# A ViT layer on one core: mean subtraction and rounding multiply of two activation quantisations moved from VectorE to GpSimd

## The reference

```python
def _act_quant(x):
    scale = 127.0 / jnp.clip(jnp.max(jnp.abs(x), axis=-1, keepdims=True), 1e-05)
    y = jnp.clip(jnp.round(x * scale), -128.0, 127.0) / scale
    return x + jax.lax.stop_gradient(y - x)

def _bitlinear(x, w):
    mu = jnp.mean(x, axis=(1, 2), keepdims=True)
    var = jnp.var(x, axis=(1, 2), keepdims=True)
    x_norm = (x - mu) * jax.lax.rsqrt(var + EPS)
    return _act_quant(x_norm) @ _weight_quant(w).T
...
q = _bitlinear(x, w_q).reshape(bsz, seq_len, NH, HD).transpose(0, 2, 1, 3)
...
return _bitlinear(out, w_o)
```

## Time and profile before

| | us |
|---|---|
| median of 3 runs | 2735.33 (2728.14 to 2740.37) |
| the profiled execution | 2730.84 |
| its span, first to last instruction | 2729.0 |
| DVE busy | 1579.2 |
| PE busy | 2267.6 |
| POOL busy | 818.9 |

### The profile page before, as it was taken

How to read it: one execution, slowest core, us unless ns; L and a number is a source line. 1 busy time by engine, 2 the same in 40 slices (tenths; PEclk the granted TensorE clock), 3 DMA queues, 4 the chain that set the end, 5 groups by cost and what they waited for, 6 DMA issues and landing times. The chain is left out here.

```text
span 2729.0 us, 46461 instructions
## 1 busy us (share of the span) xinstructions
PE 2267.6 (83%) x12048; PEld 1081.0 (40%) x12049; DVE 1579.2 (58%) x4148; ACT 1220.6 (45%) x2360; POOL 818.9 (30%) x718
## 2 busy tenths in 40 slices
PE   3798888887888888788888878878607999999998
PEld 2333333333333333333333333322204666666665
DVE  4567766676675667667666776776344333333332
ACT  1255545544454545445454544544323444444443
POOL 2112223031312313132221313212223555555554
PEclk9799889898988889789888989888758999999999
DMA  2222222222212222121222222121033333333332
GB/s 88 74 67 68 62 71 62 68 63 62 62 55 72 50 80 63 49 75 55 72 54 76 63 59 55 54 75 43 29 139 86 55 55 54 54 53 57 53 52 40
DMA packets 181078, 172.06 MB, mean 63 GB/s; under 512 B 40002, under 2 KB 169620, under 8 KB 180884
## 3 DMA queue, kind: packets, MB, share of 16 engines
q1 hardware_dynamic: 150612, 134.94, 17.2%
q0 software_dynamic: 30272, 34.80, 8.2%
HBM read 100.82 MB, written 68.93 MB: 62 GB/s over the span
## 5 line engine op out<-in xcount | busy, mean ns | idle before, releaser
L1106 DVE TENSOR_REDUCE mxs<-bank 128x1 f32<-128x512 f32 x1024 | 684.0, 686 | 476.1 <-PE bank L491 382.7
L804 ACT ACTIVATE pt<-bank 128x512 f32<-128x512 f32 x1024 | 588.2, 596 | 694.7 <-PE bank L500 634.2
L491 PE MATMUL bank<-ks,qs 96*128 96x512 bf16 x1024 | 430.4, 422 | 118.2 <-DVE mxs L1106 101.9
L500 PE MATMUL bank<-qs,ks 99*128 99x512 bf16 x1024 | 428.8, 420 | 6.6 <-ACT pt L804 5.4
L509 PE MATMUL bank<-pt,v_sb 128*32 128x512 f32 x2048 | 329.6, 721 | 0.0
L491 PEld LDWEIGHTS bank<-ks,qs 96*128 96x128 bf16 x1024 | 106.0, 104 | 496.0 <-DVE mxs L1106 344.1
L1642 POOL DMA_INDIRECT out<-y_sb,ids x136 | 215.3, 1583 | 273.2 <-DMA out<-y_sb,ids 210.7
L1688 PE MATMUL bank<-gu_h,xh 128*128 x544 | 208.2, 383 | 11.1 <-issue 7.9
L1767 DVE TENSOR_TENSOR hid_e<-bank,act_g 128x512 f32<-128x512 f32 x136 | 94.1, 692 | 210.7 <-PE bank L1688 210.7
L1771 DVE TENSOR_TENSOR hl<-bank,hh 128x512 bf16<-128x512 f32 x136 | 94.1, 692 | 210.0 <-ACT hh L1741 210.0
L966 POOL TENSOR_TENSOR cadd<-vcls,pr 128x256 f32<-128x256 f32 x64 | 40.6, 634 | 557.1 <-DVE pr L1138 556.8
(11 more groups left out here) (281 smaller groups left out, 3390.3 us busy)
## 6 DMA issues: line engine op xcount, KB each, us to landing
qs<-qk_dram SPq DMA_DIRECT2D x128, 128.0 KB, 2.4
ks<-qk_dram SPq DMA_DIRECT2D x64, 192.0 KB, 3.1
xt<-x_t SPq DMA_DIRECT2D x16, 512.0 KB, 4.1
h_dram<-h_sb SPq DMA_DIRECT2D x16, 512.0 KB, 3.4
qs<-qk_dram SPq DMA_DIRECT2D x128, 64.0 KB, 2.1
ks<-qk_dram SPq DMA_DIRECT2D x64, 128.0 KB, 3.0
hw<-h_dram SPq DMA_DIRECT2D x16, 512.0 KB, 5.6
out<-hw SPq DMA_DIRECT2D x16, 512.0 KB, 2.9
```

The lines of the kernel that those rows point to most:

```text
L491: mm(score[u % 2][:, :], qs[0:QK, h, blk(t)], ks[0:QK, h, :], start=True, stop=True) \
L500: mm(scoret[u % 2][:, :], ks[0:QK + MROWS, h, blk(t)], qs[0:QK + MROWS, h, :], start=True, stop=True).then_inc(s("pe_st"), 1)
L804: f(pt[:, t % 2, j, :], scoret[u % 2][:, :], ACT.Exp).then_inc(s("act_exp"), 1)
L1106: v.reduce_max(mxs[:, t, g * GH + j:g * GH + j + 1], score[u % 2][:, :], AX.X).then_inc(s("dve_mx"), 1)
```

## The change

The subtraction of the mean (lines 1273 and 1368) and the rounding multiplies (1285, 1394 and 1397) are taken from DVE's program and issued by POOL: at its places 13, 19, 46 and 52, each ahead of what POOL already did there. DVE signals `ms1`, `comb1` and `comb2` to POOL as it signalled others; its reductions at 15 and 49 wait for POOL's subtractions.

```diff
                     if P.ok and at == 13:
+                        hold(pool, s("dve_ms1"), 1, P, 1)
+                        hold(pool, s("act_xh"), TB, P, TB)
+                        g_.tensor_scalar(xn[:, :, :], xn[:, :, :], ms1[:, 0:1], None, ALU.subtract).then_inc(s("pool_xm"), 1)
                         rsqrt(rs1[:, :], msq1[:, 1:2], 1, 128, "dve_ve", "pool_rs", P)
                     if P.ok and at == 19:
-                        hold(pool, s("dve_q1"), TB, P, TB)
+                        hold(pool, s("dve_comb"), 1, P, 1)
+                        for t in range(TB):
+                            g_.tensor_scalar(xn[:, t, :], xn[:, t, :], comb1[:, t:t + 1], MAGIC, ALU.mult, ALU.add) \
+                                .then_inc(s("pool_q1"), 1)
+                        hold(pool, s("pool_q1"), TB, P, TB)
                         hold(pool, s("pe_xq"), 1, P, 0)
...
                     if W.ok and at == 46:
+                        hold(pool, s("dve_ms2"), 1, W, 1)
+                        g_.tensor_scalar(o_sb[:, W.par, :, :], o_sb[:, W.par, :, :], ms2[:, 0:1], None, ALU.subtract) \
+                            .then_inc(s("pool_om"), 1)
                         rsqrt(rs2[:, :], msq2[:, 1:2], 1, 128, "dve_ve2", "pool_rs2", W)
...
                     if W.ok and at == 52:
-                        hold(pool, s("dve_q2"), TB + 1, W, TB + 1)
+                        hold(pool, s("dve_comb2"), 1, W, 1)
+                        o = o_sb[:, W.par, :, :]
+                        for t in range(TB):
+                            g_.tensor_scalar(o[:, t, :], o[:, t, :], comb2[:, t:t + 1], MAGIC, ALU.mult, ALU.add) \
+                                .then_inc(s("pool_q2"), 1)
+                        cflat = oc[:, :, :].rearrange("p j d -> p (j d)")
+                        g_.tensor_scalar(cflat, cflat, comb2[0:NG, TB:TB + 1], MAGIC, ALU.mult, ALU.add) \
+                            .then_inc(s("pool_q2"), 1)
+                        hold(pool, s("pool_q2"), TB + 1, W, TB + 1)
                         hold(pool, s("pe_xqc"), 1, W, 0)
...
-                        wait(dve, s("act_xh"), TB, P, TB)
-                        v.tensor_scalar(xn[:, :, :], xn[:, :, :], ms1[:, 0:1], None, ALU.subtract).then_inc(s("dve_xm"), 1)
                     if P.ok and at == 15:
-                        wait(dve, s("dve_xm"), 1, P, 1)
+                        wait(dve, s("pool_xm"), 1, P, 1)
...
                     if P.ok and at == 18:
-                        for t in range(TB):
-                            v.tensor_scalar(xn[:, t, :], xn[:, t, :], comb1[:, t:t + 1], MAGIC, ALU.mult, ALU.add) \
-                                .then_inc(s("dve_q1"), 1)
...
-                    if W.ok and at == 48:
-                        o = o_sb[:, W.par, :, :]
-                        v.tensor_scalar(o, o, ms2[:, 0:1], None, ALU.subtract).then_inc(s("dve_om"), 1)
...
-                        wait(dve, s("dve_om"), 1, W, 1)
+                        wait(dve, s("pool_om"), 1, W, 1)
...
-                    if W.ok and at == 52:
-                        o = o_sb[:, W.par, :, :]
-                        for t in range(TB):
-                            v.tensor_scalar(o[:, t, :], o[:, t, :], comb2[:, t:t + 1], MAGIC, ALU.mult, ALU.add) \
-                                .then_inc(s("dve_q2"), 1)
-                        cflat = oc[:, :, :].rearrange("p j d -> p (j d)")
-                        v.tensor_scalar(cflat, cflat, comb2[0:NG, TB:TB + 1], MAGIC, ALU.mult, ALU.add) \
-                            .then_inc(s("dve_q2"), 1)
```

More of the change, by code:

```diff
@@ L1139, in normalise, with scales @@
             ch.end(2 * (g + 1))
-        def scales(ch, am, ax, rax, comb, aq, rs):
+        def scales(ch, am, ax, rax, comb, rs, done):
             ch(v.tensor_scalar(ax[:, :], am[:, :], rs[:, :], 1e-5, ALU.mult, ALU.max))
             ch(v.reciprocal(rax[:, :], ax[:, :]))
-            ch(v.tensor_scalar(comb[:, :], rax[:, :], 127.0, rs[:, :], ALU.mult, ALU.mult))
+            v.tensor_scalar(comb[:, :], rax[:, :], 127.0, rs[:, :], ALU.mult, ALU.mult).then_inc(s(done), 1)
         def token_stats(b, tiles_, np_, src, bn, chain, n):
@@ L1263, in body @@
                                                axis=AX.X, op=ALU.add), "dve_ms", 1, P, 1)
-                        ch = Link("dve_chain_p", 7, P)
-                        ch(v.scalar_tensor_tensor(ms1[:, :], red1[:, :], 1.0 / total, cls_f[:, 0:2], ALU.mult, ALU.add))
+                        ch = Link("dve_chain_p", 5, P)
+                        signal(v.scalar_tensor_tensor(ms1[:, :], red1[:, :], 1.0 / total, cls_f[:, 0:2], ALU.mult, ALU.add),
+                               "dve_ms1", 1, P, 1)
                         ch(v.tensor_tensor(msq1[:, 0:1], ms1[:, 0:1], ms1[:, 0:1], ALU.mult))
@@ L1271, in body @@
                                                   ALU.subtract, ALU.max))
-                        wait(dve, s("act_xh"), TB, P, TB)
-                        v.tensor_scalar(xn[:, :, :], xn[:, :, :], ms1[:, 0:1], None, ALU.subtract).then_inc(s("dve_xm"), 1)
+                        ch.end(3)
                     if P.ok and at == 15:
-                        wait(dve, s("dve_xm"), 1, P, 1)
+                        wait(dve, s("pool_xm"), 1, P, 1)
                         signal(v.tensor_reduce(out=am1[:, 0:TB], in_=xn[:, :, :], axis=AX.X, op=ALU.max,
@@ L1279, in body @@
                         wait(dve, s("pool_rs"), 1, P, 1)
-                        ch = Link("dve_chain_p", 7, P, 4)
-                        scales(ch, am1, ax1, rax1, comb1, aq1, rs1)
-                        ch.end(7)
+                        scales(Link("dve_chain_p", 5, P, 3), am1, ax1, rax1, comb1, rs1, "dve_comb")
                     if P.ok and at == 18:
-                        for t in range(TB):
-                            v.tensor_scalar(xn[:, t, :], xn[:, t, :], comb1[:, t:t + 1], MAGIC, ALU.mult, ALU.add) \
-                                .then_inc(s("dve_q1"), 1)
                         wait(dve, s("pe_aqb"), 1, P, 0)
@@ L1292, in body @@
                         ch = Link("dve_chain_c", 2, P)
+                        wait(dve, s("dve_comb"), 1, P, 1)
                         ch(v.tensor_scalar(cls_q[:, :], cls_t[:, :], ms1[:, 0:1], None, ALU.subtract))
@@ L1356, in body @@
                         signal(v.tensor_copy(ms2[:, :], d2[:, 0:2]), "dve_ms2", 1, W, 1)
-                        ch = Link("dve_chain_v", 6, W)
+                        ch = Link("dve_chain_v", 5, W)
                         ch(v.tensor_tensor(msq2[:, 0:1], ms2[:, 0:1], ms2[:, 0:1], ALU.mult))
@@ L1379, in body @@
                     if W.ok and at == 50:
-                        ch = Link("dve_chain_v", 6, W, 3)
+                        ch = Link("dve_chain_v", 5, W, 3)
                         wait(dve, s("pool_rs2"), 1, W, 1)
@@ L1386, in body @@
                                "dve_amx", 1, W, 1)
-                        scales(ch, am2, ax2, rax2, comb2, aqo, rs2)
-                        ch.end(6)
+                        scales(ch, am2, ax2, rax2, comb2, rs2, "dve_comb2")
+                        ch.end(5)
                         signal(v.tensor_scalar(aqo[:, :], ax2[:, :], 1.0 / 127.0, w_fac[:, 3:4], ALU.mult, ALU.mult),
                                "dve_aqo", 1, W, 1)
-                    if W.ok and at == 52:
-                        o = o_sb[:, W.par, :, :]
-                        for t in range(TB):
-                            v.tensor_scalar(o[:, t, :], o[:, t, :], comb2[:, t:t + 1], MAGIC, ALU.mult, ALU.add) \
-                                .then_inc(s("dve_q2"), 1)
-                        cflat = oc[:, :, :].rearrange("p j d -> p (j d)")
-                        v.tensor_scalar(cflat, cflat, comb2[0:NG, TB:TB + 1], MAGIC, ALU.mult, ALU.add) \
-                            .then_inc(s("dve_q2"), 1)
                     if P.ok and at == 50:
```

2 lines of the change are left out of this document (1 added, 1 removed).

## The result

| | before | after |
|---|---|---|
| median, both on the same chips | 2731.45 us (2727.13 to 2740.37) | 2745.18 us (2737.99 to 2758.16) |
| ratio, 95% interval | | 1.0051 (1.0029 to 1.0074) |
| profiled execution, its span | 2730.84, 2729.0 | 2741.06, 2739.2 |
| granted clock of TensorE in it | 0.892 | 0.885 |

The change makes the kernel about 14 us slower. The direction was wrong.

A forecast was written before the change was run, and what follows sets the result against it. PE, busy 83% of the span, was taken as the bound, with its waits for `qi` and `qic`. -1.2 us per image over fifteen images (-18) and +2 at the edges gave 2715 us profiled, 2719 us median; range 2692 to 2748.

The forecast's parts named there:

- How long the operations take on POOL: At the four places, a multiply on POOL takes 0.41 us (0.28 to 0.63), a subtraction 1.06 us.
- The shared resource: A DVE instruction touching only SBUF that starts inside a long POOL one ends some 0.03 us after it.
- Place 13: First subtraction: DVE's column steps end 0.9 us late, its subtraction slot of 0.67 us is saved; net +0.2 us per image.
- Places 17 to 20: First quantisation's multiplies, `comb1` to `qi`: 3.20 us becomes 3.24 us, +0.05 us per image.
- Places 46 to 49: Second subtraction: a DVE step is caught for +0.88 us, a slot of 0.66 us goes; net +0.2 us per image.
- Places 50 to 53: Second quantisation's multiplies, `comb2` to `qic`: 5.34 us becomes 3.69 us, -1.65 us per image.
- shows in the time one for one: At PE's waits for `qi` and `qic`, a change of the chain `ms` to `comb` to `qi` counts fully in the time.
- the clock recovers sooner: Rival, chance 0.15: less waiting shortens PE's half-clock stretch behind places 47 to 53, some 1.4 us per image more gained; 2698 us.
- Edges: First image at P and last at W, without attention beside them: POOL's slower operations are bare, some +2 us.
- Slow multiply: Rival, chance 0.17: POOL's multiply takes 0.63 us, so +0.6 us per image; 2747 us.
- DVE not caught: Rival, chance 0.13: DVE goes first at POOL's starts, places 13 and 47 save 0.67 us each; 2693 us.
- Gain taken back by a later wait: Rival, chance 0.13: a later wait, say for DVE, cuts the -1.65 us at place 53 to some -0.5; 2735 us.

The follow-up runs named there:

- e_fast: The change with POOL subtracting as x * 1.0 + (-mean), DVE making the negative mean in one more column step; ratio to the kernel before 1.0001.
- e_sem_only: The kernel before with all arithmetic left on DVE and only the new signals for ms1, comb1 and comb2 added; ratio to the kernel before 0.9976.
- e_fast_late: As e_fast, but POOL does `rs` first and starts its subtraction only after DVE's column steps; ratio to the kernel before 1.0003.
- e_w_mul_only: The kernel before with only the second quantisation's multiplies of the change on POOL; ratio to the kernel before 0.9959.
- e_mix: As e_fast_late, but the first quantisation's multiplies and the second's subtraction stay on DVE; ratio to the kernel before 0.9919.
- e_w_mul_waits: As e_w_mul_only, with PE's wait for qi2 and qic put behind three waits long met; ratio to the kernel before 0.9910.

## Why the prediction was wrong, point by point

- **How long the operations take on POOL: the step that failed.** The subtraction was priced at 1.06 us from rows of another pair of operations (add and multiply). It takes 2.85 us, 2.7 times as much, and the ends given for the unknown cost covered only the multiply. The range of the subtraction should have reached far higher, since no row showed its form on POOL. With 1.13 us in its place (e_fast) the ratio is 1.0001 instead of 1.0051, which is some half of the way back to the forecast's 0.994. The multiply is a pair that is fast, and was nearly right: 0.48 against 0.41 us. By the Trainium skill (GPSIMD Engine Reference, section 8) elementwise work is about twice as slow on GpSimd. Here the multiply measured 0.48 to 0.28 us, 1.7 times, which is near, and the subtraction 2.85 to 0.75, 3.8 times, which is not.
- **The shared resource.** That a step with SBUF inputs which starts beside POOL is caught was right (1.03 and 1.04 us). That it would last to POOL's end was wrong both ways: the hold ends 1.15 us after the start, and a second comes in the last 0.9 us.
- **Place 13**, +0.2 forecast: +0.57. POOL starts 0.40 us after `ms1`, not 0.18 to 0.28, and the maximum over `xn` now waits for it (starts 3.29 instead of 2.72 us after `ms1`).
- **Places 17 to 20**, +0.05: +0.21. Against e_sem_only, with the same signals, it is +0.42; the own wait that the change takes away hid half.
- **Places 46 to 49**, +0.2: +0.83. The step on `oc` +0.80, the cast with the idle time before it +0.7, the slot given back -0.66.
- **Places 50 to 53**, -1.65: `comb2` to `qic` fell from 5.22 to 3.88 us by the medians of sixteen images (5.34 was the turn that the prediction read), -1.34, of which 0.2 is the own wait.
- **The sum**: -1.2 per image forecast, +0.28 by the medians, or +4.5 us in all; added up over all the chains of the two profiled executions it is +5.4 us, nearly all of it at the edges below. The measured +13.7 us has 8 to 9 us more, with a clock of 0.881 against 0.892. That a change of the chain "shows in the time one for one" was the second step that failed: e_fast, e_fast_late and e_w_mul_only have chains 14, 21 and 25 us shorter and are 0, 0 and 11 us faster. What stood in its place is PE's own time: fewer rests and slower matmuls (in after, -9.6 and +19.8 us). The rival "the clock recovers sooner" had the right resource and, for this change, the wrong sign: of the nine kernels with the second multiplies on POOL and without additional matmuls, only e_mix and e_w_mul_waits had a higher clock than the kernel before on their chip.
- **Edges**, +2 forecast, +4.5 measured: the chains without attention beside them grew by 2.3 us (5.89 to 8.2) and 2.2 us (6.63 to 8.79).
- **The rivals.** Slow multiply: decided from 0.56 us, measured 0.48, so no. DVE not caught: no. Gain taken back by a later wait: the time it gave (2735) was nearer, but it was hardly a wait for DVE that took it. PE's three long waits for DVE's `mxs`, `cm` and `scs` come to 128.4 us before and 129.9 us after.

## What to carry to other kernels

Price an operation on another engine from a row of that very form: on GpSimd a `tensor_scalar` with one operation cost 2.5 times one that multiplies and adds, so `x * 1.0 + (-mean)` is worth writing out; `(x - mean) * 1.0` is not, it cost 3.7 us. Look at which small SBUF steps of the other engine will stand beside such an instruction, and move its start away from them. Before counting a shortened chain in full, look at TensorE's granted clock behind it, and at whether PE's busy time grows where its rests shrink. A few matmuls of no use in a rest of 1.7 us were worth 20 us in one kernel, nearly as much as the best move of work, and with the order of the waits only 6 us in the kernel before.

## What the runs showed of the hardware that was not expected

- GpSimd, 128x1024 f32: any one operation tried (subtract, add, multiply) 2.85 to 3.10 us, subtract then multiply 3.71, multiply then add 1.12, add then multiply 1.04.
- A slow GpSimd instruction of this size holds DVE's small SBUF steps in its first 1.15 us and its last 0.9 us and leaves them free between; a step with two SBUF inputs was held only by the first part, reductions by neither.
- Three waits that are long met, queued behind the one that comes last, cost PE 0.28 us; an engine's wait for its own result, 0.2 us.
- Four additional matmuls in a rest of PE turned 39 matmuls in 10.8 us into 56, and gave 0.9834, the fastest kernel here (2672.57 us, where before took 2717.76).
